# Indirect transfers paced by the attention groups, one block of eight experts, and other filler products for TensorE

## The reference

```python
exp_rank = jnp.cumsum(exp_mask.reshape(k * n, E), axis=0) - 1      # place within the expert
exp_mask = exp_mask * (exp_rank < cap)                             # cap = 1280
exp_batches = jnp.einsum('nec,nd->ecd', sec_mask, xt)              # rows to the experts
out = jnp.einsum('nec,ecd->nd', cb_weight, exp_out)                # and back, weighted
return x + attention(xn) + out
```

## Time and profile before

| | |
|---|---|
| median of 3 runs | 838.06 us (835.35 to 841.63) |
| the profiled execution | 828.99 us, of which 826.8 us are the span from first to last instruction |
| mean granted clock of TensorE | 0.812 of full |
| PE busy | 614.4 us (74%) |
| VectorE busy | 410.8 us (50%) |
| ScalarE busy | 403.2 us (49%) |
| GpSimd busy | 220.1 us (27%) |
| DMA | 60.44 MB, mean 73 GB/s |
| chain that ended last | PE 52%, another core or an unknown queue 13%, DVE 13%, ACT 10% |

### The profile page before, as it was taken

The page is one execution under the profiler, slowest core; times in us unless marked ns, Lnnn a source line. Parts: engine busy times, 40 slices in busy tenths (PEclk is TensorE's granted clock), DMA queues, the critical chain, the costliest instruction groups (busy, mean ns, idle before and its releaser), DMA issues.

```text
span 826.8 us, 9722 instructions
## 1 busy us (share of the span) xinstructions
PE 614.4 (74%) x3502; PEld 306.7 (37%) x3502; DVE 410.8 (50%) x617; ACT 403.2 (49%) x781; POOL 220.1 (27%) x222
## 2 busy tenths in 40 slices
PE   5648997101399999899989999999989510269985
PEld 3423322000133333693358535863477100022322
DVE  6758676000278888317841685158713210045742
ACT  3340365000267777637883578457745200135761
POOL 3865128777200002000010002000200777740000
PEclk9975578555579999999999999999999655555975
DMA  7883341111101014112411232111312211100011
GB/s 199 254 261 115 128 160 61 51 51 51 39 22 41 28 35 131 33 33 73 122 41 33 69 95 73 33 53 48 104 44 72 72 51 51 50 22 22 2 52 51
DMA packets 57999, 60.44 MB, mean 73 GB/s; under 512 B 8032, under 2 KB 42848, under 8 KB 57952
## 3 DMA queue, kind: packets, MB, share of 16 engines
q1 hardware_dynamic: 52160, 45.92, 18.3%
q0 software_dynamic: 5792, 13.90, 5.4%
HBM read 29.65 MB, written 29.62 MB: 72 GB/s over the span
## 4 chain that ended last, share of the span: by engine, by line
PE 52%; another core or an unknown queue 13%; DVE 13%; ACT 10%; issue 6%; SPq 3%; DMA 3%; DVEq 0%; ACTq 0%
PE bX L933 14%; PE bPV L949 14%; PE bD L1039 9%; DVE nmax L731 8%; ACT probs L585 5%; PE bD L914 4%; ACT hid L615 2%; PE bX L923 2%; DMA k_rows<-hid 2%; PE bPV L1072 2%; PE bX L1024 2%; PE bX L1028 1%; PE bX L1025 1%; PE bD L968 1%
## 5 line engine op out<-in xcount | busy, mean ns | idle before, releaser
L731 DVE TENSOR_REDUCE nmax<-bD 128x2 f32<-128x1024 f32 x256 | 301.1, 1219 | 226.4 <-remote 147.7
L585 ACT ACTIVATE probs<-bX 128x512 f32<-128x512 f32 x512 | 269.4, 597 | 249.0 <-PE bX L933 110.0
L933 PE MATMUL bX<-Q,K 27*128 27x512 f32 x512 | 196.6, 519 | 133.4 <-issue 98.8
L933 PEld LDWEIGHTS bX<-Q,K 27*128 27x128 f32 x512 | 79.2, 202 | 291.0 <-issue 146.9
L949 PE MATMUL bPV<-probs,v_aug 128*32 128x512 f32 x1024 | 158.1, 693 | 1.6 <-ACT probs L585 0.7
L914 PE MATMUL bD<-K,Q 25*128 25x512 f32 x512 | 143.5, 529 | 14.8 <-issue 4.7
L487 POOL TENSOR_TENSOR wfc_hi<-wfc,ones 128x512 fp32r<-128x512 f32 x8 | 10.2, 1275 | 355.2 <-DMA pjb<-in_pjb 355.2
L1039 PE MATMUL bD<-wpj,hid 128*128 128x128 f32 x640 | 74.0, 276 | 7.7 <-DVE xeT_lo L764 4.8
L914 PEld LDWEIGHTS bD<-K,Q 25*128 25x128 f32 x512 | 60.7, 206 | 50.3 <-DVE nmax L731 23.3
L1039 PEld LDWEIGHTS bD<-wpj,hid 128*128 128x128 f32 x640 | 72.4, 192 | 9.4 <-issue 9.4
L615 ACT ACTIVATE hid<-bX,fcb 128x512 f32<-128x512 f32 (+1 forms) x96 | 55.2, 615 | 27.4 <-PE bX L1028 26.6
(11 more groups left out here) (103 smaller groups left out, 462.6 us busy)
## 6 DMA issues: line engine op xcount, KB each, us to landing
K<-k_rows SPq DMA_DIRECT2D x128, 50.0 KB
Q<-q_rows SPq DMA_DIRECT2D x128, 48.0 KB
slot_x<-hid POOLq DMA_DIRECT2D x10, 512.0 KB, 2.9
xe<-slot_x SPq DMA_DIRECT2D x8, 640.0 KB, 4.8
slot_y<-ye SPq DMA_DIRECT2D x8, 640.0 KB, 3.7
q_rows<-hid SPq DMA_DIRECT2D x8, 512.0 KB, 3.5
k_rows<-hid SPq DMA_DIRECT2D x8, 512.0 KB, 5.1
acc<-in_x SPq DMA_DIRECT2D x8, 256.0 KB, 5.1
```

Source lines behind the costliest of these rows:

```text
L585: taken(nc.scalar.activation(probs[:, (g % 2) * 4 + i, :], next_x()[:], ACT.Exp, scale=SCALE))
L731: nc.vector.tensor_reduce(nmax[q][:, k, 2 * pair:2 * pair + 2], bank()[:], AX.X, ALU.max, negate=True).then_inc(s_dd, 1)
L933: filled(nc.tensor.matmul(next_x()[:], K[u][rows_used, q, j * P:(j + 1) * P], Q[u][rows_used, q, :], start=True, stop=True))
```

## The change

- `put_after` and `got_after` give each indirect transfer a value of the groups' counter `s_pv`, for which GpSimd waits before it issues it. The 64 scatters are spread over values 4 to 55, the 64 gathers over 69 to 124.
- All eight experts stand as one block behind the fourth group of batch 4 (`EXPERTS_AFTER = 3`, GROUPS_BEFORE = 68). The weights of experts 0 and 1 are loaded ahead, those of the others when the results of the expert two before are taken.
- The output bias is added to `acc` before the zero fills, and the fills no longer wait for the first maxima rows.
- GpSimd combines four batches, each between the third and fourth gather of the next batch; VectorE combines batches 4, 5 and 6 in groups 105, 112 and 119 and batch 7 at the end. SyncE stores the combined batches 0 to 3 earlier.
- TensorE computes six full float32 products (128 x 128 by 128 x 512, results unread) while it waits for the routing, and `keep_clock` takes three products instead of two.

```diff
@@ -58,17 +58,31 @@
 CH = [(0, 512), (512, 512), (1024, 256)]
 NCH = len(CH)
 KN = TOPK * NT
-EXPERTS_FROM, EXPERTS_TO = 2, 6
-assert 2 * (EXPERTS_TO - EXPERTS_FROM) == E
-COMBINED_BY_POOL = 2
+EXPERTS_AFTER = 3
+COMBINED_BY_POOL = 4
 N_CONST, N_LATER = 8, 3
 WR_DMAS, LOAD_DMAS, MAX_DMAS = 4, 8, 4
 ZERO_DMAS = 10
 
 D_FIRST = (LEAD + 4) * 2
 D_TURN = GB * 2 + 3
-D_EXPERTS = 2 * 2 * NCH
-D_EXPERTS_FROM = D_FIRST + EXPERTS_FROM * D_TURN + D_TURN
+D_EXPERTS_FROM = D_FIRST + EXPERTS_AFTER * D_TURN + D_TURN
+
+
+GROUPS_BEFORE = (EXPERTS_AFTER + 1) * GB + 4
+
+
+def put_after(i):
+
+    return 4 + i * (GROUPS_BEFORE - 16) // KN
+
+
+def got_after(i):
+
+    return GROUPS_BEFORE + 1 + i * (B * GB - GROUPS_BEFORE - 4) // KN
+
+
+COMBINED_AT = {GROUPS_BEFORE + 9 + 7 * b: b for b in range(COMBINED_BY_POOL, B - 1)}
...
+            def load_expert(e):
+                q = e % 2
+                sp.dma_start(wfc[q][:], c_fc[e]).then_inc(s_w[q], 16)
+                sp.dma_start(wpj[q][:], c_pj_v[e]).then_inc(s_w[q], 16)
+                sp.dma_start(fcb_s[q][:], fcb[e]).then_inc(s_w[q], 16)
+                sp.dma_start(pjb_s[q][:], pjb[e].to_broadcast([P, C])).then_inc(s_w[q], 16)
+
+            def experts():
                 sp.wait_ge(s_put, KN * 16)
-                load_rows(e)
-                for q in range(2):
-                    sp.dma_start(wfc[q][:], c_fc[e + q]).then_inc(s_w[q], 16)
-                    sp.dma_start(wpj[q][:], c_pj_v[e + q]).then_inc(s_w[q], 16)
-                    sp.dma_start(fcb_s[q][:], fcb[e + q]).then_inc(s_w[q], 16)
-                    sp.dma_start(pjb_s[q][:], pjb[e + q].to_broadcast([P, C])).then_inc(s_w[q], 16)
-
-            def experts(b):
-                e0 = b * 2 - 2 * EXPERTS_FROM
-
-                before = (b - EXPERTS_FROM) * (D_TURN + D_EXPERTS) + D_EXPERTS_FROM
-                sp.wait_ge(s_dd, before + NCH)
-                load_rows(e0 + 1)
-                for q in range(2):
-                    sp.wait_ge(s_dd, before + (3 + q) * NCH)
-                    sp.dma_start(slot_y_v[e0 + q], ye[:]).then_inc(s_slot, 16)
+                load_rows(0)
+                for e in range(E):
+                    if e < E - 1:
+                        sp.wait_ge(s_dd, rows_item(e, NCH - 1) + 1)
+                        load_rows(e + 1)
+                    sp.wait_ge(s_dd, results_end(e))
+                    sp.dma_start(slot_y_v[e], ye[:]).then_inc(s_slot, 16)
+                    if e + 2 < E:
+                        load_expert(e + 2)
...
+                if b == B - 2:
+                    sp.wait_ge(s_x, x_filled(b, 3))
+                    take_pool(0, 2)
                 if last:
                     max_rows(1, 0, m)
                     max_rows(1, 1, m + 1)
+                    take_pool(2, COMBINED_BY_POOL)
...
+            pool.wait_ge(s_xn, B)
+            nc.gpsimd.tensor_tensor(acc[:], acc[:], bo_s[:, None, :].to_broadcast([P, NT, C]), ALU.add).then_inc(s_bo, 1)
             pool.wait_ge(s_fill, 7)
-            pool.wait_ge(s_nq[0], MAX_DMAS * 16)
             for h in range(ZERO_DMAS):
                 pool.dma_start(slot_x.rearrange("(p h r) c -> h p (r c)", p=P, h=ZERO_DMAS)[h], hid_f[:, 0:per]
                                ).then_inc(s_zero, 16)
                 pool.wait_ge(s_zero, h * 16 + 16)
-            nc.gpsimd.tensor_tensor(acc[:], acc[:], bo_s[:, None, :].to_broadcast([P, NT, C]), ALU.add).then_inc(s_bo, 1)
-            pool.wait_ge(s_xn, B)
             for k in range(TOPK):
                 for n in range(NT):
                     col = k * NT + n
+                    pool.wait_ge(s_pv, put_after(col))
                     pool.indirect_dma_start(slot_x, bass.IndirectOffsetOnAxis(ap=put_i[:, col:col + 1], axis=0),
                                             xn_all[:, n, :], None, bounds_check=SLOTS - 1, oob_is_err=False
                                             ).then_inc(s_put, 16)
...
+            for e in range(E):
+                q = e % 2
+                pool.wait_ge(s_w[q], e // 2 * 64 + 64)
...
+            pool.wait_ge(s_slot, E * 16 + 16)
+            for b in range(B):
+                for k in range(TOPK):
+                    for n in range(TT):
+                        col = k * NT + b * TT + n
+                        pool.wait_ge(s_pv, got_after((b * TOPK + k) * TT + n))
+                        pool.indirect_dma_start(gathered(b, k * TT + n), None, slot_y,
+                                                bass.IndirectOffsetOnAxis(ap=get_i[:, col:col + 1], axis=0),
+                                                bounds_check=SLOTS - 1, oob_is_err=False).then_inc(s_get[b], 16)
+                        if 0 < b <= COMBINED_BY_POOL and (k, n) == (0, 2):
+                            combine(b - 1)
 
...
+                if b * GB + g in COMBINED_AT:
+                    combine(COMBINED_AT[b * GB + g])
...
-                    if last and g >= GB - 4:
-                        combine(g - GB + 4 + COMBINED_BY_POOL)
                 if last:
+                    dve.wait_ge(s_dd, d.value())
                     normalise(1)
-                    combine(B - 2)
                     take_out(b)
-                    dve.wait_ge(s_dd, d.value())
                     combine(B - 1)
...
+                chunks = [rows_in(0, c) for c in range(NCH)]
+                for e in range(E - 1):
+                    up(e, chunks)
+                    chunks = []
+                    for kind, c in BETWEEN:
+                        if kind == "rows":
+                            chunks.append(rows_in(e + 1, c))
+                        else:
+                            down(e, c)
+                up(E - 1, chunks)
                 for c in range(NCH):
-                    down(e0 + 1, 1, c)
+                    down(E - 1, c)
...
+            pe.wait_ge(s_lo, 2 * B)
+            for _ in range(6):
+                nc.tensor.matmul(bPV[:], ident[:], rows(xn_all, B - 1).rearrange("p n c -> p (n c)"), start=True, stop=True)
             pe.wait_ge(s_prefix, 1)
             pe.wait_ge(s_xT, B)
             pe.wait_ge(s_hot, 1)
-            pe.wait_ge(s_lo, 2 * B)
             hot_f = hot[:].rearrange("p n e -> p (n e)")
...
-                        keep_clock(2)
+                        keep_clock(3)
```

More of the change, by code:

```diff
@@ L89, in x_filled @@
     n = b * GB + g
-    experts_before = sum(n > (turn + 1) * GB + 3 for turn in range(EXPERTS_FROM, EXPERTS_TO))
+    experts_before = E * HC * NCH if n >= GROUPS_BEFORE else 0
     attn_turned = (n - 2) // GB if n >= 2 else 0
-    return 1 + 4 * (n + 1) + (n + 3) // 4 + attn_turned + 2 * HC * NCH * experts_before
+    return 1 + 4 * (n + 1) + (n + 3) // 4 + attn_turned + experts_before
 def maxima_taken(m):
@@ L378, in turn @@
                 if with_experts:
-                    load_experts(b)
+                    for e in range(2):
+                        load_expert(e)
                 sp.wait_ge(s_x, x_filled(b, 15))
@@ L383, in turn, with put_out, take_pool @@
                 if with_experts:
-                    experts(b)
-            each_turn(turn)
-            for b in (*range(COMBINED_BY_POOL, B - 1), *range(COMBINED_BY_POOL), B - 1):
-                if b < COMBINED_BY_POOL:
-                    sp.wait_ge(s_comb_p, b + 1)
-                else:
-                    sp.wait_ge(s_comb, b + 1 - COMBINED_BY_POOL)
-                sp.dma_start(rows(out_v, b), rows(acc, b)).then_inc(s_out, 16)
+                    experts()
+            def put_out(b):
+                sp.dma_start(rows(out_v, b), rows(acc, b)).then_inc(s_out, 16)
+            def take_pool(start, stop):
+                for b in range(start, stop):
+                    sp.wait_ge(s_comb_p, b + 1)
+                    put_out(b)
+            each_turn(turn)
+            for b in range(COMBINED_BY_POOL, B):
+                sp.wait_ge(s_comb, b + 1 - COMBINED_BY_POOL)
+                put_out(b)
             sp.wait_ge(s_out, B * 16)
@@ L602, in sums, with experts @@
                 nc.scalar.copy(pv_s[:], bPV[:]).then_inc(s_pvo, 1)
-            def experts(b):
-                before = (b - EXPERTS_FROM) * (D_TURN + D_EXPERTS) + D_EXPERTS_FROM
-                for q in range(2):
-                    e = b * 2 - 2 * EXPERTS_FROM + q
+            def experts():
+                for e in range(E):
+                    q = e % 2
                     for c, (c0, w) in enumerate(CH):
-                        at = NCH + BETWEEN.index(("rows", c)) if q else c
-                        act.wait_ge(s_d, before + at + 1)
-                        nc.scalar.copy(xeT[0][:, c0:c0 + w], bD[(before + at) % 2][:, 0, 0:w]).then_inc(s_xhi, 1)
+                        item = rows_item(e, c)
+                        act.wait_ge(s_d, item + 1)
+                        nc.scalar.copy(xeT[0][:, c0:c0 + w], bD[item % 2][:, 0, 0:w]).then_inc(s_xhi, 1)
                     for hc in range(HC):
```

76 lines of the change are left out of this document (29 added, 47 removed).

## The result

The changed kernel takes 715.2 us (median of 4 runs, 710.4 to 717.3), the kernel before 839.9 (4 runs, 835.4 to 865.6) beside it: a ratio of 0.852, 95% interval 0.846 to 0.859. The profiled execution took 716.1 us. The forecast was 680, the range 648 to 725. Medians here are of all runs; ratios and their intervals leave out the executions more than 1.5% above the fastest of their kernel.

The account below looks back on a forecast made before the run. Dense rows of indirect transfers were taken to stop attention. 829 less 178.3 left 650.7; +17 burst, -7 prologue, +3.6, +6 and +2 experts, +4.6 combining gave 677 profiled, 680 as median; range 648 to 725.

Parts of the forecast that it names:

- Transfers spread: Scatters and gathers under attention: pacing them by groups removes the whole 178.3 us loss, with isolated transfers taken as free.
- Rival 1: Indirect transfers: each costs a fixed time whatever the density, so no change (838 us); 6% whole, 9% in part.
- rival 2: Indirect transfers: each holds TensorE's signals until the next one, 2.4 us each, 967 us in all; chance 6%.
- First scatters still a burst: After the zero fills: 12 to 14 scatters due at once cause one stop, 13 us plus 4 at half clock: +17.
- Rival 3: First scatters: the burst doesn't end itself, scatters stay dense, only the gathers' 90.9 us are won, 747 us; chance 5%.
- Prologue: Before the first group: six products and packs of three keep the clock up, 12 score pairs get faster: -7 us.
- Eight experts as one block: Expert block: 162.0 us against 158.4 for four pairs (+3.6), row waits +6, first rows late +2.
- Combining: VectorE combining inside attention: the first two batches lie mostly on the path, +4.6 us; the third costs 0.
- The 3 us added from the profiled execution to the median: Whole kernel: about half of the 1.1% by which the median stood above the profiled execution, taking 677 to 680 us.

Follow-up runs that it names:

- puts_dense: The changed kernel with all 64 scatters allowed from the first on, gathers still paced, on chip 4: 807.5 us, ratio 0.952 to the kernel before.
- puts_later: The changed kernel with scatters allowed from the 13th group on, one for each 0.75 groups, on chip 2: 700.2 us.
- gets_unpaced: The changed kernel with all 64 gathers allowed from the first on, scatters still paced, on chip 5: 706.2 us.
- puts_unpaced: The changed kernel with all 64 scatters allowed from the first on, gathers still paced, on chip 5: 694.3 us.
- rows_first: The changed kernel with the next-but-one expert's rows asked for ahead of the results' store and the weight loads, on chip 2: 676.5 us.
- after_again: The changed kernel itself, unedited, run once more on chip 4: 713.0 us, ratio 0.848 to the kernel before.
- combine_late: The changed kernel with VectorE combining batches 4 to 6 in the last batch's groups 12 to 14, on chip 2: 701.2 us.
- spaced_again: The kernel before with one small awaited fill on GpSimd behind each indirect transfer, on chip 13: 730.0 us, ratio 0.862 to the kernel before.

## Why the prediction was right, and where it was off

The forecast was 677 us for a profiled execution; it took 716.1. The mechanism, transfers spread so that the attention runs on under them, was right. That the time lies in the range is in part luck: its upper end was made for a price of each transfer, which did not come, and what filled it was a queue's order and half clock behind short pauses. Four of the signs that the prediction named did not show: the clock at 1.0 from the stop to the last batch, about 168 us for the experts, waits of 0 to 3 us on their rows, and a first group near 85 us. By the steps:

- *Transfers spread, 178.3 us at no price for each.* Right. 47.3 us for a batch under paced scatters and under paced gathers is what a batch took before without any. Rival 1 (cost by number) and rival 2 (each transfer holds signals) are out; puts_dense against the changed kernel shows it, one edit apart on one chip. But of the four chips it is worth something on three. The prediction took the stop for a property of the kernel; it depends on something else too, the chip or the occasion.
- *First scatters still a burst, +17.* Right in mechanism and nearly in size: 13 scatters in a row, 15.8 us (72.2 less the 56.4 of puts_later, whose stretch has full clock). Behind the stop the scatters that wait for a group come 4.06 us apart (145.84 and 149.90) instead of 2.96 a group, until the clock is back at 160; an estimate from that is 5 us for the half clock, 4 forecast, and 11 for the stop, 13 forecast. Rival 3, a burst that does not end itself, is out.
- *Prologue, -7.* Wrong: the first group came at 93.1 instead of 92.5, so +7.6 against the term. Stretches of the changed kernel:

```profile
57.00:60.00 3.00, 3.00 (x8) 1.32 (x9) 2.83 (x6) 0.65 (x1) 2.94 (x5) 1.00 0.88 268
66.00:69.00 3.00, 1.10 (x3) 0.67 (x4) 3.00 (x7) 0.00 (x0) 2.04 (x2) 0.83 0.97 287
75.00:78.00 3.00, 3.00 (x8) 1.38 (x9) 1.85 (x4) 0.00 (x0) 2.45 (x10) 0.50 0.00 0
87.00:90.00 3.00, 3.00 (x10) 1.67 (x10) 1.78 (x2) 0.00 (x0) 1.36 (x2) 0.75 0.40 157
```

  The six products held the clock at 1.00, but behind the routing TensorE waits again (busy 1.10 of 3.00 from 66 to 69) and the clock falls there; then packs of three run at half clock and cost more than packs of two. The clock comes back at 88. First groups at 87.0, 87.0, 91.2, 91.7, 91.8, 93.5, 94.6, 96.2 and 98.5 us in the other profiles of kernels with this prologue, around the 92.5 of before: on the whole it brings nothing to the first group. What follows it varies more. In six of the ten profiles the first groups run at full clock (in the kernel before it came at 113 us), in four the clock was at half under them for 34 us or more. That can cost as much as the burst: 70.0 us for the first stretch in gets_unpaced, which has no stop but half clock from 100 to 137 us, against 56.3 in puts_unpaced on the same chip, and 85.6 in rows_first, which has a short row of scatters as well. The prediction allowed 5 us for this case. The Trainium skill (TensorE: Matmul & The Clock Gate, What's actually happening) says that activity releases the throttle; that agrees at last, at 88 us, and does not say why TensorE, busy 18.00 of 18.00 us from 69 on here and 23.00 of 23.00 from 69 on in the kernel before, stayed at 0.50 all that time.
- *Eight experts as one block, 170 us.* Mis-sized: 192.5. The step that failed is the order in SyncE's queue: 1 us of wait for each of six experts was taken, 0 to 3 allowed, 3.6 measured (21.5 in all), because the transfer took 6.3 us beside store and weights and was issued 3.6 us behind the store. The larger miss is that the pause has a second price that the sum did not name: 15.2 us of products at half clock. Without the wait the block takes 155.8, less than the 162.0 worked out and a little less than the four pairs of before (158.4).
- *Combining, +4.6.* Mis-sized by the same omission: 15.3 in the late stretch (7.6 in after_again, where the clock came back sooner). The third combining, at group 119, starts at 670 us, behind that stretch, and costs nothing that can be seen: the last batch takes 49.2 us with it and 49.3 in combine_late without it.
- The last batch took 1.5 us more, the first groups 2.2 less at full clock. Together: 7.6 + 22.5 + 10.7 + 1.5 - 2.2 - 1.2 (burst) = 38.9 of the 39.1 us.
- The 3 us added from the profiled execution to the median were not there (716.1 and 715.2).

The rule of the Trainium skill that a DMA cannot be slowed by a compute operation and the other way round (SBUF — State Buffer, SBUF: two separate sides) is about ports. As a rule for the engines' time it does not hold here: on chip 4 a row of indirect transfers kept TensorE to 4.17 us of 40. Through what, no run shows. Three instructions of the kernel before, inside its first stop, narrow it down:

```profile
158.68 0.79 PE L933 MATMUL bX<-Q,K 27*128 27x512 f32 x1
...
165.25 0.60 ACT L585 ACTIVATE probs<-bX 128x512 f32<-128x512 f32 x1 [7.04 <-issue]
...
165.90 0.79 PE L933 MATMUL bX<-Q,K 27*128 27x512 f32 x1 [6.43 <-issue]
```

A product that starts at 158.68 should free ScalarE within a microsecond, and ScalarE goes on at 165.25; what ScalarE finishes at 165.85 starts TensorE's next product at 165.90. The delay lies between TensorE's product and the engine that waits for it; the way back takes 0.05 us. In puts_dense the same happens on a larger scale: a product starts at 155.78, and ScalarE goes on at 192.23. What holds it, and why chip 5 is free of it, stays open. The gathers alone were paced or not only on chip 5; that a pause helps them too is suggested by spaced_again, which has no stop under them either.

## What to carry to other kernels

Look at a row of indirect transfers as a load on the other engines: if waits without a releaser begin some transfers into it, a pause of less than a microsecond between them, or a wait for a counter of the work beside them, may be worth more than anything else in the kernel, but time both kernels on more than one chip before you believe it. Where TensorE runs under full load, price each new pause twice, as the wait and as the stretch at half clock that may stand behind it (3 to 10 us of half clock after pauses of some 3.6 us in the experts, 7 us in one execution and 37 in another after 1.4 us in the attention). In a queue that issues in order, ask for what is wanted next before storing what is done.

## What was not expected of the hardware

- The same kernel takes 839 to 841 us (medians) on three chips and 671 on a fourth, each used on one occasion; 64 transfers, one each 1.28 us, stop TensorE on the former and not on the latter.
- A transfer each 1.97 us stops nothing on a chip where the kernel before takes 839.
- The clock fell after a pause of 1.40 us and came back only some 37 us of attention groups later; in another execution of the same kernel, after 1.42 us, it was back after 7. In the experts, with full 128 x 128 products, it was back within about 10 us.
- The stop outlasts a row of transfers, and by more the longer the row is: 8.8 us after 64 scatters, on two occasions, and 1.8 to 2.7 after 8 to 13.
